# Splitting 2048 columns in eight pieces on GpSimd, and another order of the eight short maxima units, in a two-layer attention kernel

## The reference, cut to what matters

```python
qkv = x @ Wqkv                        # x is layernormed and modulated: 2 batches, 2048 tokens, 256 columns
qkv_rows -> heads                     # reshaped, not transposed: 32 query heads of 16, 8 key and value heads
scores = einsum('bhqd,bhkd->bhqk', q, k) / sqrt(16)
scores = where(causal, scores, -inf)
aw = softmax(scores, axis=-1)
aw = aw[:, :, 0] - lam * aw[:, :, 1]  # pairs of heads are subtracted
attn = einsum('bhqk,bhkd->bhqd', aw, v) * (1 - LAMBDA_INIT)
```

## Time and profile before

| quantity | value |
|---|---|
| three runs | 2374.82 us (median), 2372.23 to 2375.65 |
| the profiled execution | 2382.39 us, span 2380.7 us |
| PE busy | 2161.4 us, 91% |
| DVE busy | 1834.1 us, 77% |
| ACT busy | 1582.7 us, 66% |
| POOL busy | 594.2 us, 25% |
| mean granted clock of TensorE | 0.935 of full speed |

### The profile page before, as it was taken

One profiled execution on the slowest core, in us unless ns is written; L12 is line 12 of the kernel. 1 busy time (PEld: TensorE's weight loads), 2 busy tenths in 40 slices (PEclk: granted clock), 3 DMA queues, 4 the chain that ended last, 5 costly groups with the idle time before them and its releaser, 6 DMA issues. The chain is left out here.

```text
span 2380.7 us, 43994 instructions
## 1 busy us (share of the span) xinstructions
PE 2161.4 (91%) x15852; PEld 882.1 (37%) x15852; DVE 1834.1 (77%) x4663; ACT 1582.7 (66%) x3201; POOL 594.2 (25%) x716
## 2 busy tenths in 40 slices
PE   6799999999999999999999999999999889889983
PEld 5132323232332323232323232333222268567831
DVE  3888888888888888888888888888889258334467
ACT  2167777877777777777777778777777735246633
POOL 1213131313223131312221313132211124100067
PEclk8599999999999999999999999999999989899955
DMA  5220302121120202030303031211200020000001
GB/s 156 39 48 6 68 13 61 25 49 33 40 46 27 48 26 48 31 67 6 68 6 68 12 62 23 51 31 43 40 6 2 18 82 0 1 1 1 1 22 49
DMA packets 95985, 84.63 MB, mean 36 GB/s; under 512 B 48544, under 2 KB 81440, under 8 KB 95776
## 3 DMA queue, kind: packets, MB, share of 16 engines
q1 hardware_dynamic: 95776, 81.91, 15.5%
HBM read 26.81 MB, written 16.78 MB: 18 GB/s over the span
## 5 line engine op out<-in xcount | busy, mean ns | idle before, releaser
L726 ACT ACTIVATE probs<-b_bank 128x512 f32<-128x512 f32 (+1 forms) x2304 | 1177.2, 577 | 412.8 <-PE b_bank L879 404.5
L578 DVE TENSOR_REDUCE m_part<-a_bank 128x1 f32<-128x512 f32 x1536 | 970.4, 683 | 120.2 <-PE a_bank L863 114.1
L879 PE MATMUL b_bank<-q_pack,k_pack 64*128 64x512 bf16 (+7 forms) x5120 | 934.1, 352 | 17.4 <-ACT probs L726 14.5
L863 PE MATMUL a_bank<-k_pack,q_pack 64*128 64x512 bf16 (+3 forms) x2560 | 822.3, 361 | 95.9 <-DVE m_part L578 65.2
L911 PE MATMUL acc<-probs,v_tile 128*32 128x512 f32 (+3 forms) x5120 | 600.3, 551 | 3.1 <-POOL probs L437 0.8
L575 DVE CUSTOM_DVE_ANT_0 a_bank<-a_bank,mask_a 128x128 f32<-128x128 f32 (+3 forms) x1024 | 481.0, 515 | 124.8 <-PE a_bank L863 122.3
L879 PEld LDWEIGHTS b_bank<-q_pack,k_pack 64*128 64x128 bf16 (+1 forms) x5120 | 290.2, 95 | 555.3 <-ACT probs L726 426.3
L863 PEld LDWEIGHTS a_bank<-k_pack,q_pack 64*128 64x128 bf16 x2560 | 223.4, 94 | 422.6 <-DVE m_part L578 224.2
L437 POOL TENSOR_SCALAR_AFFINE_SELECT probs<-probs 128x512 f32<-128x512 f32 (+1 forms) x192 | 151.6, 789 | 906.2 <-ACT probs L726 904.2
L911 PEld LDWEIGHTS acc<-probs,v_tile 128*32 128x32 f32 x5120 | 108.4, 108 | 192.1 <-issue 111.3
L575 DVE DVE_READ_ACCUMULATOR2_ANT m_part<- 128x1 f32 x1024 | 144.9, 141 | 0.0
(11 more groups left out here) (191 smaller groups left out, 1824.9 us busy)
## 6 DMA issues: line engine op xcount, KB each, us to landing
q_pack<-part SPq DMA_DIRECT2D x384, 64.0 KB, 2.3
k_pack<-part SPq DMA_DIRECT2D x192, 64.0 KB, 2.3
scratch<-qkv_row SPq DMA_DIRECT2D x16, 512.0 KB, 2.8
heads<-scratch SPq DMA_DIRECT2D x16, 512.0 KB, 3.7
xg<-in_L_attn_x SPq DMA_DIRECT2D x16, 256.0 KB, 2.8
scratch<-qkv_row SPq DMA_DIRECT2D x32, 128.0 KB, 2.7
q_pack<-m_rows SPq DMA_DIRECT2D x256, 2.0 KB
x<-in_L_attn_x SPq DMA_DIRECT2D x4, 1024.0 KB, 11.9
```

The lines of the kernel that those rows point to most:

```text
L578: dve.tensor_reduce(out, bank[:, 0:w], AX.X, ALU.max).then_inc(a_maxed, 1)
L726: act.activation(probs[:, n % P_RING, h, at:C], b_bank[bank_no(("B", n, h))][:, at:C], ACT.Exp, scale=HD ** -0.5) \
L863: pe.matmul(a_bank[at % A_RING][:, 0:w], q_pack[buf][rows, hp, 0, q:q + P], k_pack[buf][rows, 0, C * c:C * c + w], start=True, stop=True). ...
L879: ins = pe.matmul(b_bank[bank_no(slot)][:, at:at + C - q], k_pack[par][rows, n2, P * kt:P * (kt + 1)], q_pack[par][rows, h // 2, n2, C * j ...
```

## The change

It has two independent parts. GpSimd's three subtractions of 2048 columns become eight times three of 256 columns, one piece in each of the program steps 22 to 29. Only the first piece has a wait for `part0_ready`, and only the last tells that the parts are ready. The split ahead of the loop stays whole. And block 0's eight units, which had widths 128, 128, 256, 256, 384, 384, 512, 512, now have 128, 512, 128, 512, 256, 384, 256, 384.

```diff
-A_UNITS = [(j, t, c, hp) for j in range(NJ) for t in range(TB) for c in range(j + 1) for hp in range(QH // 2)]
+A_UNITS = [(0, t, 0, hp) for ts in ((0, 3), (1, 2)) for hp in range(QH // 2) for t in ts]
+A_UNITS += [(j, t, c, hp) for j in range(1, NJ) for t in range(TB) for c in range(j + 1) for hp in range(QH // 2)]
...
-NORMALISE_AT, DEVIATION_AT, CENTRE_AT, GATHER_AT, SPLIT_AT = 0, 1, 3, 14, 22
+NORMALISE_AT, DEVIATION_AT, CENTRE_AT, GATHER_AT = 0, 1, 3, 14
+PIECES = 8
+SPLIT_AT = range(22, 22 + PIECES)
...
+        def rest_count(n, i):
+
+            return 2 * (n + 1) if n < 2 else 4 + 2 * PIECES * (n - 2) + 2 * (i + 1)
...
-            def split(n):
-
-                pool.wait_ge(part0_ready, upto(n + 1))
-                if not (isinstance(n, int) and n == 0):
-                    pool.wait_ge(packs_in, upto(16 * PACK_DMAS * n))
-                pool.tensor_tensor(rest[0:80, :], headT[0:80, :], part[0][0:80, :], ALU.subtract).then_inc(rest_ready, 1)
-                pool.tensor_tensor(part[1][0:80, :], headT[0:80, :], part[0][0:80, :], ALU.subtract).then_inc(rest_ready, 1)
-                pool.wait_ge(rest_ready, upto(2 * (n + 1)))
-                pool.tensor_tensor(part[2][0:80, :], rest[0:80, :], part[1][0:80, :], ALU.subtract).then_inc(parts_ready, 1)
+            def split(n, i, pieces):
+
+                cols = slice(S // pieces * i, S // pieces * (i + 1))
+                if i == 0:
+                    pool.wait_ge(part0_ready, n + 1)
+                    if n:
+                        pool.wait_ge(packs_in, 16 * PACK_DMAS * n)
+                pool.tensor_tensor(rest[0:80, cols], headT[0:80, cols], part[0][0:80, cols], ALU.subtract).then_inc(rest_ready, 1)
+                pool.tensor_tensor(part[1][0:80, cols], headT[0:80, cols], part[0][0:80, cols], ALU.subtract).then_inc(rest_ready, 1)
+                pool.wait_ge(rest_ready, rest_count(n, i))
+                ins = pool.tensor_tensor(part[2][0:80, cols], rest[0:80, cols], part[1][0:80, cols], ALU.subtract)
+                if i == pieces - 1:
+                    ins.then_inc(parts_ready, 1)
...
-                    if s == SPLIT_AT:
-                        split(g + 2)
+                    if s in SPLIT_AT:
+                        split(g + 2, s - SPLIT_AT[0], PIECES)
```

More of the change, by code:

```diff
@@ L406, in inverse_deviation @@
                 pool.tensor_tensor(rstd[:, :], veps[:, :], expo[:, 0:2], ALU.pow).then_inc(rstd_ready, 1)
-            def split(n):
-                pool.wait_ge(part0_ready, upto(n + 1))
-                if not (isinstance(n, int) and n == 0):
-                    pool.wait_ge(packs_in, upto(16 * PACK_DMAS * n))
-                pool.tensor_tensor(rest[0:80, :], headT[0:80, :], part[0][0:80, :], ALU.subtract).then_inc(rest_ready, 1)
-                pool.tensor_tensor(part[1][0:80, :], headT[0:80, :], part[0][0:80, :], ALU.subtract).then_inc(rest_ready, 1)
-                pool.wait_ge(rest_ready, upto(2 * (n + 1)))
-                pool.tensor_tensor(part[2][0:80, :], rest[0:80, :], part[1][0:80, :], ALU.subtract).then_inc(parts_ready, 1)
+            def split(n, i, pieces):
[10 more added lines that the diff above has]
+                    ins.then_inc(parts_ready, 1)
             inverse_deviation(0)
             inverse_deviation(1)
-            split(1)
+            split(1, 0, 1)
             def gather_heads(n):
```

## The result

The changed kernel takes 2334.56 us (median of four runs, 2331.56 to 2337.59) against 2375.24 for the kernel before (2372.23 to 2378.99). The ratio is 0.983 with a 95% interval of 0.981 to 0.985, so it is 36 to 46 us faster. The forecast was 2328, within 2314 to 2344. A second timing of it gave 0.981 (0.979 to 0.984).

What follows compares the result with a forecast made beforehand. PE, at 91% of the span, lost time in step 26 to DVE's waits for GpSimd. Gains of 14 x (3.58 - 0.65) = 41.0 and 15 x 0.4 = 6.0 us, off 2374.8, gave 2328, range 2314 to 2344.

Steps and rivals of the forecast that it cites:

- The stall and its cause: Step 26, groups 0 to 13: two DVE instructions end with GpSimd's, costing 2.2 us of the 3.58 lost a group.
- Nothing paces GpSimd to its steps: Steps 24 to 29: 18 GpSimd instructions of 0.65 us run behind the output work, from about 654.1 to 666.
- The rival of a train that lets VectorE in nowhere: Step 25's negation waits for all 18 GpSimd instructions, 11 us for 2.2, giving about 2492 us; chance 0.04.
- The remaining wait: Step 26: both DVE instructions wait half a piece's instruction, 0.33 us each, 0.65 a group, bounds 0 and 1.3.
- The clock's part: Step 26: PE's clock at 0.50 for 3.4 us costs 1.4 us a group, counted as gone.
- The order: Steps 15 to 18, block 0's units: 0.4 us a group, bounds -0.3 and 0.8, 15 times, 6.0 us.
- VectorE's idle time of 0.97 us ahead of a tile of 256: Block 0: this 0.97 us should go, with shorter waits before 128 and 256 in its place.
- The sum: Whole kernel: 41.0 us from step 26 and 6.0 us from block 0's units, 47.0 us in all.

## Why the prediction was right, and where it was not

**The stall and its cause: right.** The two negations end with a GpSimd instruction in all five settings (4.08 us at either place, 2.13, 1.16 and 0.67), and last 0.17 us each where there is none. Where the clock stayed at full, step 26 is 3.08 us plus the delay of VectorE, within 0.01 us: 3.43 with 0.34, 3.66 with 0.57, 4.94 with 1.85. That the two engines' instructions exclude each other, and that the stall is as long as what is left of GpSimd's instruction, is shown by these runs; that ports are the reason is not. The rule of the Trainium skill (SBUF — State Buffer, section "SBUF: two separate sides") is that the shared ports are locked for one whole instruction, and all of these durations agree with it.

**Nothing paces GpSimd to its steps: right.** The six later pieces ran in one train behind the output work, and the whole split, put in step 27, began in step 25. The last piece ended at 651.70, 21.3 us after the first had begun, as the 644.9 to 666 of the working had it. The rival of a train that lets VectorE in nowhere fell with it: the negation began inside one of these pieces and ended with that one.

**The remaining wait: on the safe side.** I had put 0.65 us a group for both waits, half an instruction each. They are 0.28 and 0.06 us, and the gain in step 26 is 45.3 us in place of 41.0. The instruction's length was right (0.67 against 0.65). Where in it the negation falls could not be known ahead; it was one number for all groups, as expected.

**The clock's part: right.** With waits of 0.34 us it no longer fell in step 26, in none of 14 groups.

**The order: the term that was mis-sized.** I had 0.4 us in each of 15 groups, 6.0 in all. Undisturbed, a group gains 0.31 (12.24 to 11.93), and over all 15 it is 2.5 us. The working was wrong before any run: its own terms, 0.6 less in step 15, 0.3 more in step 17 and 0.1 to 0.2 more in step 18, leave 0.1 to 0.2 and not 0.4. That the undisturbed 0.31 comes near 0.4 is luck. Timed from the first score matmul of each step, step 15 went from 3.06 to 2.46 us, as laid out; step 16 from 2.83 to 2.55, for which there was no term; step 17 from 3.28 to 3.41, a loss of 0.13 and not 0.3; and step 18 from 3.07 to 3.51. (Step 15 of group 4 begins at 621.95; the 2.93 us in the earlier trace rows leave out its first 0.12.) The loss in step 18 is the larger error: its second unit waits for the bank of a 384 tile that PE hands over only after the transposes of step 17, as the run with the third unit in step 16 showed. This is the wait in the changed kernel:

```profile
617.05 0.39 PE L874 MATMUL a_bank<-k_pack,q_pack 64*128 64x512 bf16 x1 [0.28 <-DVE m_part L586]
```

VectorE's idle time of 0.97 us ahead of a tile of 256, which was to go, came back as 0.88 ahead of the later pair of 256, in step 17.

And in five groups (5, 7, 10, 11 and 13) the four steps took 12.14 to 12.51 us, 1.9 us more in sum than at 11.93: there the negation of block 3's maxima meets GpSimd's copy of the gathered heads (L437, 1.25 us), as in group 5, VectorE first and then GpSimd:

```profile
716.88 0.63 DVE L601 TENSOR_SCALAR m_neg<-m_max 128x16 bf16<-128x16 f32 x1
```

```profile
716.23 1.25 POOL L437 COPY heads_by_j<-heads 128x1280 f32<-128x1280 f32 x1 [0.78 <-DMA heads<-scratch]
```

This happened before as well, up to a negation of 1.22 us in group 5, but cost nothing there: all of the groups 0 to 13 took 12.23 to 12.25 us, since VectorE was waiting for PE in step 15 anyway. The new order took that cover away. With the copy paced, too, these groups are like the others.

**The sum: nearer than its parts.** The profiled spans differ by 47.3 us, and the forecast was 47.0, but that is partly luck. The 47.3 are 45.3 in step 26 (41.0 forecast), 2.5 in steps 15 to 18 (6.0 forecast) and 3.0 from two fewer falls of the clock in step 20, which the sum counted at nothing, less 3.5 elsewhere. Of these, 1.0 is in step 27, and 2 come behind the groups, in stages that the change does not touch; in the twelve profiles of all versions the time from the start of the last group's last step to the end varies between 488.1 and 491.6 us. The medians of the runs differ by 41, with 36 to 46 as the interval, so the median came out 6.6 us above the forecast. The profiled execution of before lay 7 us above its median, that of after 2 us above its own. Why they did stays open.

## What to carry to other kernels

The place of an instruction in the program sets no time: here, without a wait, GpSimd's work ran as soon as what stood ahead of it was done, and met a small instruction of VectorE. Where two engines exclude each other, first look for a wait that orders them. Here such a wait lengthened no step, and it left step 26 0.35 us a group shorter than the eight pieces did; in the time that difference did not stand clear of the noise by itself. Before changing an order, look at which collisions its slack is hiding.

## What was not expected of the hardware

Not every VectorE instruction on SBUF, the memory that both engines work on, waits. In the kernel before, the reduction of the maxima (L583, SBUF to SBUF) ran inside GpSimd's L416 in 0.19 us, and the reciprocal (L620) at 652.38 inside L414 in 0.25, while the negation in the same L416 took 2.17:

```profile
654.31 0.19 DVE L583 TENSOR_REDUCE m_max<-m_part 128x16 f32<-128x32 f32 x1
```

GpSimd's subtraction of 80 partitions costs 0.67, 1.16, 2.13 and 4.08 us for 256, 512, 1024 and 2048 columns: about 0.19 us fixed and 1.90 ns a column, so eight pieces cost GpSimd (8 x 0.67 - 4.08) x 3 = 3.8 us a group, all of it under idle time.

The clock of TensorE falls in step 20 in some groups and not in others, with the same instructions and waits ahead: in four groups of 14 before, in two and in three in two profiles of the changed kernel, in none with the eight pieces and the old order and in none with four pieces. In the twelve profiles it fell in none to four of the 14 groups, with either order. At 1.5 us each this is as large as what the order of the units was meant to bring, and it may be why gains seen in the windows of steps did not show in the time of two versions (the third unit in step 16, and the paced waits in the old order); each had four falls in its profile. What decides it was not settled.
